# In layer 0 of a four-layer graph network, VectorE takes the residual of the second half one step later

## The reference

```python
q = x @ Wq.T + bq; k = x @ Wk.T + bk; v = x @ Wv.T + bv      # 4 heads of 32
scores = clip(q . k / sqrt(32), -10, 10)                     # per chunk of 128 keys
scores = where(mask == 0, -10, scores)
attn = softmax(scores, over the 128 keys of a chunk)
ctx = sum over the 8 chunks of attn @ v                      # 1024 x 128
out = ctx @ Wo.T + bo + x                                    # output projection, residual
out = layernorm(out) * gamma + beta                          # second normalisation
```

## Time and profile before

| | |
|---|---|
| median of 3 runs | 1999.77 us (1999.49 to 2002.91) |
| the profiled execution | 1999.09 us |
| span in its trace | 1997.2 us |
| mean granted TensorE clock | 0.924 of full speed |
| layer 0 in the trace | up to about 660 us |
| period of a block from residual to residual | 72 to 75.5 us |

### The profile page before, as it was taken

How to read it: one execution, slowest core, us unless ns; L and a number is a source line. 1 busy time by engine, 2 the same in 40 slices (tenths; PEclk the granted TensorE clock), 3 DMA queues, 4 the chain that set the end, 5 groups by cost and what they waited for, 6 DMA issues and landing times. The chain is left out here.

```text
span 1997.2 us, 36885 instructions
## 1 busy us (share of the span) xinstructions
PE 1644.5 (82%) x13620; PEld 1053.7 (53%) x13620; DVE 1601.0 (80%) x2710; ACT 1338.3 (67%) x1751; POOL 134.9 (7%) x131
## 2 busy tenths in 40 slices
PE   3988888898886677999999768876787668999997
PEld 1444443444433456777777556665665454455454
DVE  3888998998898457888889889898989866766764
ACT  2776576676664476777776888888988825545543
POOL 1001111111010000000000000000000000000000
PEclk9999999999998588999999878888988879999999
DMA  8645635635622311111111121122123200000000
GB/s 230 157 110 127 138 94 119 148 89 128 144 72 72 121 43 43 44 43 42 42 48 49 53 68 65 65 65 65 65 80 97 96 23 1 11 22 11 11 11 21
DMA packets 74923, 146.50 MB, mean 73 GB/s; under 512 B 11937, under 2 KB 34722, under 8 KB 74754
## 3 DMA queue, kind: packets, MB, share of 16 engines
q1 hardware_dynamic: 74754, 144.23, 26.3%
HBM read 101.85 MB, written 8.78 MB: 55 GB/s over the span
## 5 line engine op out<-in xcount | busy, mean ns | idle before, releaser
L1241 ACT ACTIVATE g<-s_all,steep_d 128x1024 fp8e4<-128x1024 f32 x608 | 642.3, 1135 | 38.8 <-DMA s_all<-s_rows 21.6
L600 ACT ACTIVATE e<-s_ps 128x1024 f32<-128x1024 f32 x256 | 248.3, 1023 | 23.0 <-PE s_ps L450 18.4
L1325 DVE TENSOR_TENSOR g<-g,edge 128x1024 int32<-128x1024 int32 x192 | 227.9, 1220 | 31.8 <-ACT g L1241 31.7
L1176 PE MATMUL acc<-arena,g 128*128 128x102 bf16 (+1 forms) x3072 | 209.5, 229 | 17.8 <-DVE sums L1332 14.1
L1176 PEld LDWEIGHTS acc<-arena,g 128*128 128x128 fp8e4 x3072 | 201.2, 100 | 35.5 <-issue 27.2
L760 DVE SCALAR_TENSOR_TENSOR e<-e,bound 128x1024 f32<-128x1024 f32 x160 | 191.2, 1229 | 32.5 <-ACT e L600 32.2
L1176 PE MATMUL acc<-parts,g 128*128 128x102 bf16 (+1 forms) x3072 | 208.6, 228 | 6.3 <-DVE sums L1332 6.3
L1176 PEld LDWEIGHTS acc<-parts,g 128*128 128x128 fp8e4 x3072 | 200.3, 99 | 21.5 <-issue 13.0
L446 PE MATMUL s_ps<-qs,ks 128*128 128x512 f32 x512 | 194.6, 490 | 7.0 <-DMA ks<-split 5.4
L462 PE MATMUL sum_ps<-e,pick 128*32 128x256 f32 x2048 | 139.3, 390 | 67.0 <-DVE e L760 60.0
L2031 ACT ACTIVATE z<-z,shift 128x1024 f32<-128x1024 f32 x64 | 73.5, 1149 | 169.4 <-DVE shift L2099 169.4
(11 more groups left out here) (189 smaller groups left out, 2417.2 us busy)
## 6 DMA issues: line engine op xcount, KB each, us to landing
s_all<-s_rows SPq DMA_DIRECT2D x96, 512.0 KB, 3.7
inv_all<-inv_rows SPq DMA_DIRECT2D x256, 128.0 KB, 2.9
qs<-split SPq DMA_DIRECT2D x128, 128.0 KB, 3.2
ks<-split SPq DMA_DIRECT2D x128, 128.0 KB, 3.2
x<-in_x SPq DMA_DIRECT2D x8, 512.0 KB, 6.6
inv_rows<-inv SPq DMA_DIRECT2D x32, 128.0 KB, 1.7
adj_in<-in_adj SPq DMA_DIRECT2D x8, 512.0 KB, 4.3
out_x<-x SPq DMA_DIRECT2D x8, 512.0 KB, 3.2
```

The costliest lines, as they stand in the source:

```text
L600: act.activation(e[:, 2 * (i % 2) + hp, :, :], s_ps[:, hp, :, :], ACT.Exp, scale=SCALE).then_inc(exp_done, 1)
L1176: ins = pe.matmul(self.acc[:, bank, o:o + self.NS], self.g[:, h % RING, jt, it * P:(it + 1) * P], self.upper[par][:, jt, h, :, :].rearrang ...
L1241: act.activation(self.g[:, h % RING, jt, :], self.s_all[:, h % 2, :], ACT.Relu, bias=self.steep_d[par][:, jt, h:h + 1], scale=STEEP, satur ...
L1325: dve.tensor_tensor(both, both, c.edge[:, some, :].rearrange("p t n -> p (t n)").bitcast(I32), ALU.bitwise_and).then_inc(self.g_ready, 1)
```

## The change

The residual of the second half of the graph before is called at the end of VectorE's step 11 and no longer at the end of its step 10. Nothing else is edited: TensorE still projects at step 10, ScalarE normalises at step 13, VectorE updates at step 14.

```diff
                     if not first:
                         if i == 2:
                             update(b - 1, 0)
-                        elif i == 10:
+                        elif i == 11:
                             residual(b - 1, 1 - par, 1, True)
                         elif i == 14:
                             update(b - 1, 1)
```

## The result

The changed kernel takes 1973.26 us (median of 4 runs, 1971.59 to 1977.64) against 1999.74 us before (1999.49 to 2002.91), a ratio of 0.9867 with a 95% interval of 0.9847 to 0.9888. It is 26.5 us faster. The profiled execution took 1971.73 us, its span is 1969.9 us, 27.3 us less than before.

A forecast was written before the change was run, and what follows sets the result against it. No engine is full, so the order of waits between VectorE and TensorE bounds the kernel. Waits of 16.3 and 6.2 us less 1.0 for loads give 21.5 us, 1999.1 to 1977.6, stated as 1978 us; range 1973.5 to 1987.

The forecast's parts named there:

- VectorE's wait is on the path, and TensorE waits for VectorE: Ahead of the late residual, seven blocks of layer 0: the projection wait, 16.3 us in all, delays the whole loop.
- The 0.68 us ahead of the inversion goes as well: Step 12, VectorE: the wait for sums(11) ahead of the inversion vanishes, 6.2 us over seven blocks.
- New waits for the loads, 1.0 us: Step 11, loads of `inv_all`, reached earlier by VectorE: 0.6 us in block 7, 0.2 in block 6; 1.0 us taken off.
- rival (a): Inverse store or loads queue behind key copies and land late, losing 7 to 9 us: 1985 to 1987 us, chance 0.12.
- TensorE's idle time replaced by 1 to 1.5 us ahead of `sums(12)`: Sign of being right: TensorE's 3.81 us ahead of sums(11) gone, 1 to 1.5 us ahead of sums(12) instead.
- ScalarE, GpSimd and the update have slack: Behind the later residual, steps 13 and 14: 1.0 us of slack plus 0.8 us at VectorE, delay costed at nothing.
- The copy of `late`: GpSimd's copy in six blocks, moved beside step 13's weighing: same 0.41 us slowing, term 0; other bound a 2.5 us gain.
- Behind layer 0 the other layers start when it ends: After layer 0: the later layers start when it ends, so layer 0's gain of 21.5 us is the whole sum.
- a scatter of a few us, as the runs of before (3.4 us apart) do: Whole kernel: clocks of the later layers add a few us of scatter to the forecast time.
- rival (d): More gain: the copy of `late` slows nothing, 2.5 us, and loads come in time, 1.0 us: 1974.5 us, chance 0.08.

The follow-up runs named there:

- both_at_11: The changed kernel with TensorE's projection also moved, from step 10 to step 11: 1987.91 us, ratio 0.9932 to the kernel before.
- residual_at_12: The changed kernel with the late residual one step later, at the end of step 12, projection left at step 10: 2000.53 us, ratio 1.0007 to the kernel before.
- copy_at_inversion: The kernel before with GpSimd's copy of `late` held until VectorE's first clip of step 12 is done: 1998.97 us, ratio 0.9988.
- copy_at_weighing: The changed kernel with GpSimd's copy of `late` held until both clips of step 12 are done, measured twice: 1980.22 and 1980.51 us.
- the repeats: The changed kernel measured twice more without any edit: 1971.88 us (ratio 0.9853) and 1968.91 us (ratio 0.9855).
- projection_before_scores: The kernel before with TensorE's second-half projection of step 10 placed ahead of scores(11) instead of behind it: 1994.6 us, ratio 0.9975.

## Why the prediction was wrong, and where it was right

- *VectorE's wait is on the path, and TensorE waits for VectorE*: right. The wait is gone in all seven blocks, and the period of a block from late residual to late residual fell by 3.0 to 3.6 us. Moving the projection along (both_at_11) gives more than half of the gain back, moving the residual one step further (residual_at_12) all of it.
- *The 0.68 us ahead of the inversion goes as well*: right in mechanism and size. All 6.2 us ahead of the inversion of step 12 are gone; 0.4 us came back ahead of the other inversions, so 5.8 are measured.
- *New waits for the loads, 1.0 us*: right, 1.3 us, at step 11 of block 7, none at step 15. A wait of over 1 us there was named as a sign of rival (a). It is one wait, in the block that prepares no next graph and so has no key copies in the queue: the sum's own 0.6 us of block 7 grown, not (a).
- *TensorE's idle time replaced by 1 to 1.5 us ahead of `sums(12)`*: nearly; 0.88 us stand there and 0.9 us more than before ahead of `sums(13)`.
- *ScalarE, GpSimd and the update have slack*: right at step 11, and residual_at_12 shows the edge one step further.
- *The copy of `late`: "I take the same 0.41 ... So the term is 0"*: this is the step of the sum that failed. Of its two bounds (the copy slows nothing in its new place, or costs the same 0.41 us) the sum took the wrong one. The copy came to lie beside the weighing in block 5 only, where it cost 0.4 us as reckoned. In the five others GpSimd's two operations ahead of it were 0.8 us shorter in their new place, so the copy ran beside the inversion (385.19 in block 4) and slowed nothing. The clips of step 11 gained 0.41 us in six blocks, so the term is 2.5 - 0.4 = 2.1 us and not 0. With it the sum is 16.3 + 5.8 - 1.3 + 2.1 = 22.9 us, and layer 0's stretch measured 23.6. In the kernel before, most of this contention was given back as waits for TensorE in the one profile that took it away (copy_at_inversion); in the changed kernel, where no such wait follows, its return costs 0.23 us a block (copy_at_weighing).
- *"Behind layer 0 the other layers start when it ends"*: the sum so put what comes from outside the stretch at nothing. It was 3.7 us in the profiled execution, only 0.3 of them in layers 1 and 2, and by the medians 3 us in the result and 5 to 6 us in the repeats. In the repeats' profiles layers 1 and 2 are 3.2 and 2.3 us shorter than in the kernel before (919.9 and 920.8 against 923.1).
- *"a scatter of a few us, as the runs of before (3.4 us apart) do"*: too small. 49 more executions of the kernel before lie 12.8 us apart, and even the median of the changed kernel moved from 1973.26 to 1968.91 us over three measurements. The range had 1 us of room below rival (d).

Against the sum of 21.5 us, layer 0 gave 2.1 us more and the rest of the program 2.9 us by the medians; from the rounded forecast of 1978 us that is the 4.7 us. Rival (d), 1974.5 us, came nearest, and half of it came true: the copy slows next to nothing, but the loads did not come in time. What stays open is why the rest of the program was faster each time. The mean granted clock goes with the time of an execution (0.926 and 0.918 in the fastest and slowest ten of the kernel before), but what decides it, and whether the moment at which layers 1 and 2 start has a part in it, no run here shows.

## What to carry to other kernels

Put a consumer that stands in an in-order queue where its producer is certainly done, and fill the hole in front of it with work that is already free; but look one step further too, since one step later the next consumer (ScalarE here) had no slack left and all of the gain was lost. Before counting a wait as time, ask what the engine that waits for you does after idling: in one profile TensorE came out of a 2.87 us hole at half speed, and 5.2 of 7.9 us of shortened waits came back elsewhere. A saving of 1% in one stage came here with 0.15 to 0.3% of the total from outside that stage, and executions of one kernel lay 0.6% apart; so let the range hold that, and profile more than one execution before a difference of a few us is given a cause.

## What was not expected of the hardware

- GpSimd is hit harder by the contention than VectorE: its copy of 128x512 took 0.61 us beside the inversion and 1.61 us beside clips with two SBUF operands, its root of 128x4 took 1.01 us while VectorE was idle, 1.38 beside a masked clip and the inversion, and 2.04 beside the weighing. The two clips of 1.2 us each lost 0.41 us together, an instruction of the weighing 0.29 to 0.41. The Trainium skill, GPSIMD Engine Reference, table of specifications, names exactly these partners, VectorE instructions with two SBUF inputs or in a two-port mode; the traces agree for two SBUF inputs. For the masked clip, a tensor_scalar, no slowing of it beside the root was seen (0.69 and 0.68 us).
- TensorE's sums took 1.07 us at a granted clock of 0.98 to 1.00, and 1.93 us behind 2.87 and 4.28 us of idle time at a granted clock of 0.50 (1.2 against 2.4 GHz); but behind 3.81 us in block 4 of the kernel before they still took 1.07 us and the values after them 1.81, at 0.50. Behind the same 2.87 us in projection_before_scores they took 1.93 us in three blocks and 1.07 in one. The idle time alone does not tell which matmul is hit.
- An idle stretch of 2.8 to 3.1 us stands ahead of VectorE's first clip of block 4 in all thirteen profiles, where the same clip of block 5 waits at most 1.3 us. The profile puts it down to ScalarE's exponentials in ten of them and to issue in three; here are the kernel before, the changed one and copy_at_inversion:

```profile
341.52 1.23 DVE L760 SCALAR_TENSOR_TENSOR e<-e,bound 128x1024 f32<-128x1024 f32 x1 [2.83 <-ACT e L600]
```

```profile
330.65 1.23 DVE L760 SCALAR_TENSOR_TENSOR e<-e,bound 128x1024 f32<-128x1024 f32 x1 [3.06 <-ACT e L600]
```

```profile
342.41 1.23 DVE L761 SCALAR_TENSOR_TENSOR e<-e,bound 128x1024 f32<-128x1024 f32 x1 [2.83 <-issue]
```

  In the changed kernel the clip starts 2.9 us after the exponentials it needs have begun (327.79), in block 5 1.05 us after (399.97), and one of them takes 1.0 us. So they do not explain it; its cause is open. Since it is nearly as long in every kernel, it has next to no part in the differences between them.
